# Moving routing and key rounding within the instruction orders of a fused attention and expert kernel

## What is computed

```python
x = x + xattn(layernorm(x), ctx)      # x (4,256,128), ctx (4,1601,128)
x = x + moe(layernorm(x))
# xattn: scores = clip((xWq+bq)(cWk+bk)^T / sqrt(128), -100, 100); softmax(scores) (cWv+bv)
# moe, 8 experts, top 2 of the softmax over the router's logits:
gu = einsum('th,ehn->ten', flat, gate_up_proj) + gate_up_bias      # n = 512
gate, up = minimum(gu[..., :256], 7), clip(gu[..., 256:], -7, 7)
act = (up + 1) * gate * sigmoid(1.702 * gate)
down = einsum('tei,eih->teh', act, down_proj) + down_bias
out = (down of the top 2 experts * their probabilities).sum()
```

## Time and profile before

| | |
|---|---|
| Runs | 161.22 us median of 3 (161.13 to 161.69) |
| Profiled execution | 162.93 us, its span 161.2 us |
| TensorE busy | 150.5 us, 93% of the span, granted clock 0.989 in the mean |
| VectorE, ScalarE, GpSimd busy | 100.9, 100.6, 49.8 us |
| Chain that ended last | TensorE 77%, VectorE 7%, ScalarE 7%, GpSimd 4% |

### The profile page before, as it was taken

How to read it: one execution, slowest core, us unless ns; L and a number is a source line. 1 busy time by engine, 2 the same in 40 slices (tenths; PEclk the granted TensorE clock), 3 DMA queues, 4 the chain that set the end, 5 groups by cost and what they waited for, 6 DMA issues and landing times.

```text
span 161.2 us, 3023 instructions
## 1 busy us (share of the span) xinstructions
PE 150.5 (93%) x1004; PEld 136.7 (85%) x1004; DVE 100.9 (63%) x288; ACT 100.6 (62%) x205; POOL 49.8 (31%) x49
## 2 busy tenths in 40 slices
PE   7899799999999699999949999799999999999993
PEld 7779699999999599989839888688888888887982
DVE  0678769295958485820983499376664576642774
ACT  3283878836476545768823671699777777787550
POOL 1265549043026400300081770333332123333030
PEclk9999999999999999999987999999999999999999
DMA  4979999500000000000000000000000000000022
GB/s 113 374 294 398 389 400 361 157 4 0 0 2 4 0 0 0 4 0 0 2 0 4 0 0 0 0 4 0 2 0 0 0 0 0 0 4 0 4 65 65
DMA packets 5909, 10.69 MB, mean 66 GB/s; under 512 B 380, under 2 KB 3080, under 8 KB 5896
## 3 DMA queue, kind: packets, MB, share of 16 engines
q1 hardware_dynamic: 4968, 10.00, 17.2%
q10 hardware_dynamic: 928, 0.53, 1.2%
HBM read 10.00 MB, written 0.52 MB: 65 GB/s over the span
## 4 chain that ended last, share of the span: by engine, by line
PE 77%; DVE 7%; ACT 7%; POOL 4%; DMA 2%; issue 2%; DVEq 0%; ACTq 0%
PE T L1120 18%; PE S L917 12%; PE S L918 11%; PE S L919 11%; PE O L1014 10%; PE T L998 6%; DMA x_sb<-in_x 2%; ACT pr L418 2%; POOL rstd L286 2%; PE S L1120 1%; ACT pT L426 1%; ACT ct_hi L409 1%; DVE sc L630 1%; DVE xn L591 1%; POOL ct_lo L324 1%
## 5 line engine op out<-in xcount | busy, mean ns | idle before, releaser
L819 DVE TENSOR_SCALAR up<-up 128x512 f32<-128x512 f32 x32 | 15.0, 470 | 29.9 <-ACT up L503 29.9
L349 POOL TENSOR_TENSOR x<-x,xn 128x512 f32<-128x512 f32 x13 | 17.3, 1328 | 38.8 <-ACT xn L523 38.8
L917 PE MATMUL S<-x_hi,w_hi 128*128 128x512 f32 x64 | 26.8, 419 | 1.2 <-ACT keysT_sb L497 1.2
L426 ACT ACTIVATE pT<-T 128x512 f32<-128x512 f32 (+1 forms) x32 | 15.4, 512 | 20.0 <-PE T L998 19.9
L523 ACT ACTIVATE xn<-T,w_scaled 128x128 f32<-128x128 f32 x56 | 16.0, 373 | 17.4 <-PE T L1120 12.3
L1014 PE MATMUL O<-pT,ctx_sb 128*128 128x128 f32 (+1 forms) x208 | 25.9, 276 | 0.2 <-ACT pT L426 0.2
L630 DVE TENSOR_SCALAR_CACHE_REDUCE sc<-S,clip_hi 128x400 f32<-128x400 f32 (+1 forms) x32 | 19.1, 631 | 10.0 <-PE S L919 9.8
L918 PE MATMUL S<-x_lo,w_hi 128*128 128x512 f32 x64 | 25.3, 395 | 0.0
L919 PE MATMUL S<-x_hi,w_lo 128*128 128x512 f32 x64 | 25.3, 395 | 0.0
L1014 PEld LDWEIGHTS O<-pT,ctx_sb 128*128 128x128 f32 (+1 forms) x208 | 24.6, 192 | 0.6 <-ACT pT L426 0.5
L497 ACT ACTIVATE keysT_sb<-S,gate_bias 128x512 f32<-128x512 f32 x32 | 22.7, 708 | 1.7 <-PE S L919 1.7
(11 more groups left out here) (127 smaller groups left out, 245.2 us busy)
## 6 DMA issues: line engine op xcount, KB each, us to landing
keysT_sb<-in_ctxT SPq DMA_DIRECT2D x3, 801.0 KB, 10.0
ctx_sb<-in_ctx SPq DMA_DIRECT2D x3, 768.0 KB
gu_sb<-in_gu SPq DMA_DIRECT2D x1, 2048.0 KB, 15.0
ctx_sb<-in_ctx SPq DMA_DIRECT2D x3, 256.0 KB, 4.6
x_sb<-in_x ACTq DMA_DIRECT2D x1, 384.0 KB, 5.2
keysT_sb<-in_ctxT SPq DMA_DIRECT2D x1, 289.0 KB, 5.6
out_x<-xn SPq DMA_DIRECT2D x1, 256.0 KB, 2.3
out_x<-xn SPq DMA_DIRECT2D x2, 128.0 KB, 1.8
```

The lines of the kernel that those rows point to most:

```text
L349: nc.gpsimd.tensor_tensor(acc, acc, y_sb[:, k % 2, :], ALU.add).then_inc(y_added, 1)
L426: nc.scalar.activation(pT[0:rows, t0:t0 + m, :].rearrange("p t q -> p (t q)"), T[bank][0:rows, 0:m * P], ACT.Copy).then_inc(t_free[bank], 1)
L917: nc.tensor.matmul(dst, a_hi, b_hi, start=True, stop=False)
```

## The change

Three lists of instructions are reordered; no instruction is added or taken away. In ScalarE's and GpSimd's lists batch 3's key parts are made one query tile earlier. In VectorE's list half 0's comparison and weights move ahead of the first expert's first clip, the products of step 0 move up among the residual and its moments, step 1's clips and products surround the last split of x2, and half 1's comparison and weights come in one piece ahead of step 3, which becomes a plain `expert` call.

```diff
@@ -333,8 +333,8 @@
             keys_lo(2, 1)
             root2(0)
             keys_lo(3, 0)
+            keys_lo(3, 1)
             root2(1)
-            keys_lo(3, 1)
             root2(2)
             root2(3)
             for b in range(HALF // TPB, BATCHES):
@@ -470,14 +470,14 @@
             copies(2)
             exponentials(3)
             split_x2(0)
+            keys_hi(3, 0)
             copies(3)
             exponentials(4)
             copy_oT(1)
-            keys_hi(3, 0)
+            keys_hi(3, 1)
             copies(4)
             exponentials(5)
             split_x2(1)
-            keys_hi(3, 1)
             copies(5)
             exponentials(6)
             copy_oT(2)
@@ -843,22 +843,23 @@
             split_x2(last - 1)
             invert_sums(last)
             route_probabilities(0)
-            clip_ups(0, 0, 0)
             route_compare(0)
             route_weights(0)
+            clip_ups(0, 0, 0)
+            product(0, 0, 0)
+            residual(last)
+            residual_moments(last)
             clip_ups(0, 0, 1)
+            product(0, 0, 1)
+            normalise(xn2, x1, mv2, rstd2, last * TPB, TPB, rstd2_ready, BATCHES, xn2_ready)
             add_router_bias(last - 1)
-            residual(last)
             logit_maximum(last - 1)
-            residual_stats(last)
             logit_differences(last - 1)
-            residual_mean(last)
-            residual_variance(last)
-            product(0, 0, 0)
-            normalise(xn2, x1, mv2, rstd2, last * TPB, TPB, rstd2_ready, BATCHES, xn2_ready)
-            product(0, 0, 1)
-            expert(1, 1)
+            clip_ups(1, 1, 0)
+            product(1, 1, 0)
+            clip_ups(1, 1, 1)
             split_x2(last)
+            product(1, 1, 1)
             add_router_bias(last)
             logit_maximum(last)
             logit_differences(last)
@@ -866,14 +867,9 @@
             sum_exponentials(1)
             invert_exponentials(1)
             route_probabilities(1)
-            clip_ups(3, 3, 0)
-            product(3, 3, 0)
             route_compare(1)
-            clip_ups(3, 3, 1)
-            split_w_hi(3, 1, 4)
-            product(3, 3, 1)
-            split_w_lo(3, 1)
             route_weights(1)
+            expert(3, 3, split=3)
             with dve.Fori(1, PAIRS - 1) as i:
                 for k in range(4):
                     e, h = PAIR_STEPS[k]
```

## The result

The changed kernel takes 157.64 us in the median of 4 runs (157.42 to 157.82), against 161.41 (161.13 to 161.69) for the kernel before in the same comparison: a ratio of 0.9766, with an interval of 0.9742 to 0.979. The profiled execution took 157.56 us with a span of 155.8 us.

What follows compares the result with a forecast made beforehand. TensorE, busy 93% of the span, was taken as the bound, so only its waits and slow clock could pay. 1.5 + 4.3 - 0.5 = 5.3 us off the median 161.2 gave 155.9; range 154.5 to 157.9.

Steps and rivals of the forecast that it cites:

- Part A: Attention stage, batch 3's key parts made earlier: TensorE's wait for GpSimd and the refill go, gain 1.50 us.
- Part B: First half's routing and products before the first down projection: two waits and the slow clock go, gain 4.3 us.
- Part C: Second half's routing ahead of expert step 3: SiLU wait goes, GpSimd's addition causes a new pause, loss 0.5 us.
- Rival 1: New pause ahead of step 3's down projection makes the clock fall, about 1.7 us more: 157.6 us; chance 0.30.
- Rival 2: GpSimd's addition doesn't hold step 3's second product: 1.2 us less, 154.7 us; chance 0.12.
- Rivals 3 and 4: Step 0: residual's wait delays half 1's product, 157.9, chance 0.05; GpSimd's powers hold expert 1's products, 158.1, chance 0.03.
- Rival 5: After the new pause at step 3 the clock doesn't come back: above 180 us if through the rest; chance 0.02.

Runs made afterwards that it cites:

- part A alone: Only batch 3's key parts made earlier, against the kernel before: median 160.46 us, ratio 0.9866.
- the short addition: Changed kernel with step 2's addition on GpSimd cut from 512 columns to 8, the rest of that sum left out: 156.46 us.

## Why the prediction was right, and where its size was off

The direction and each wait came out as worked; the forecast for the median, 155.9, was 1.7 us too low (157.64), about a third of the forecast gain. The sum made against the profiled execution was 157.6 us with a span of 155.9; the profiled execution of the changed kernel has 157.56 and 155.8.

- **Part A, 1.50.** The profile shows 1.51 (3.23 less 1.72), the three executions with the key parts alone at full clock 1.7. Cover and order were as described.
- **Part B, its instructions.** With part A's gain of 1.5 put back, half 1's product ended at 80.3 (forecast 80.4), the normalisation started at 80.2 (80.46) and the router at 83.8 (83.85). GpSimd's powers held nothing: a product at 80.16 lasts 0.69 inside the power at 79.86. (The working has one slip of addition, 77.35 for 77.33, without effect.)
- **Part B, its price.** Here the prediction was off. It split the 4.3 us into 2.2 of waiting and some 2.0 of slow clock, and then counted both against the median of the runs. The step that failed is "The runs without that overhead have their median at 161.22, as long as the span: 161.2 - 5.3". There is no such overhead. The gap of 1.7 us between the profiled execution and the median was the slow clock itself: 38 of 63 executions of the kernel before don't have it. In those B is worth 2.4 to 2.6 (161.3 less 157.19, less A's 1.5 to 1.7), and the whole change 3.7 instead of 5.3. The term of the sum that was mis-sized is the slow clock: 1.6 (162.93 less 161.3) to 2.0 in the profiled execution, nothing in the median. In the typical execution at 0.989 it is 1.4 us, less than the 2.0 read from the rows; where the difference of 0.4 to 0.6 goes was not followed. The equality of a span with a median should have been a warning, for in the same row the profiled execution's own time was 1.7 above its span.
- **Part C, loss of 0.5.** 0.45 by the kernel without it. The hold was forecast for the rounding; rounding and product came as worked (96.37 is 102.2 in the old clock, for 102.3), the pause of 1.72 us for 1.95 too.
- **Rival 1** (the new pause makes the clock fall) ends at nearly the measured time, 157.6, but for a reason that isn't there: all ten executions of the changed kernel kept the clock. **Rival 2** (no hold, 154.7) is out by the trace and by the short addition. **Rivals 3 and 4** are out by the products' times. **Rival 5** didn't occur.

That the range held the time was luck in this respect: its upper end, 157.9, stood there for rivals 1 and 3, not because the doubt about the median had been seen.

Open: what decides whether the clock falls in an execution of the kernel before, and for how long. It fell in 25 of 63 executions, and with part A alone in 3 of 6; in the three of these that left a trace, at or just behind the two pauses that are 2.2 us together. It did not in the ten of the changed kernel, with a pause of 1.7 in one piece, nor in the six of the kernel with the first routing moved alone, with one of 1.24 there. Six are few: at a rate of 25 in 63 a row of six without a fall comes up once in twenty. The Trainium skill ("TensorE: Matmul & The Clock Gate", section "HAM oscillation") ties a fall to a gap longer than any in these kernels; the fall behind 2.2 us in two pieces shows that this is not the only way to it.

## What to carry to other kernels

Before a profiled execution's time is set against a median, take the span from the time, in every execution that lists both: where the difference is constant, an odd microsecond between executions is real, and it is to be looked for in the granted clock of each. What removes a pause behind which the clock sometimes falls also removes that spread.

An instruction list in order is a place to fill: work without a taker belongs where the engine idles anyway, and the product that TensorE waits for belongs ahead of the bookkeeping. When a step is moved up, ask which engine's work it releases and on what that lands: here earlier weights released a scaling, that an addition on GpSimd, and that held the rounding ahead of the very product for which TensorE then waited.

## What the runs showed of the hardware

- GpSimd's addition of 128x512 (1.26 us) holds VectorE's next operation that reads two operands from SBUF, or clips or rounds within SBUF, until it ends: the rounding took 1.51 us instead of 0.42, products 1.57 and 1.82 instead of 0.69, and the clip of rows 10 took 1.46 instead of 0.43. Cut to 8 columns (0.20 us) it left the rounding at 0.44. Where such an operation of VectorE was first, by 0.02 us, it kept its time and the addition took 1.81. A power of 128x16 (3.01 us) held nothing: a product inside it took 0.69. The Trainium skill ("SBUF — State Buffer", section "SBUF: two separate sides") has the first to start keep the shared ports for its whole instruction. The additions agree; the power doesn't.
- The same program was granted the full clock in 38 executions; in 17 and 8 others the mean was 0.989 and 0.967 to 0.969, at a cost of 1.4 and 4.1 us. In the traces kept this was one stretch at half the clock behind two pauses of 0.97 and 1.24 us, and in one of the 8 TensorE was busy without a gap for 9.5 us of it. Without that pair of pauses the clock fell in none of 64 executions.
